# Down product with features on rows, row maxima on VectorE, in a LoRA feed-forward kernel

## The chip, the cores and the metric

One Trainium2 chip (trn2), one core. The metric is device time in microseconds (us). A core has TensorE (PE: matmuls from SBUF into PSUM), VectorE (DVE), ScalarE (ACT), GpSimd (POOL) and SyncE (SP, which here only starts transfers), each with its own instruction queue, working in order and meeting through semaphores.

## What is computed

`x` has 128 entries of 32 tokens with 512 features. Each entry has a LoRA index. Cut to what matters:

```python
gate = x @ W_gate.T + lora(x, A_gate, B_gate)     # 512 -> 1376, rank 16, by entry
up   = x @ W_up.T   + lora(x, A_up,   B_up)
act  = silu(gate) * up
down = act @ W_down.T + lora(act, A_down, B_down) # 1376 -> 512
amax = clip(max(abs(down), axis=-1), 1e-5)        # one value per token
out  = (down / amax) @ levels[weight_2bit].T * (amax * weight_scale) + bias
return x + out
```

The indices are sorted at run time, and the branch that this input takes treats tiles of 512 tokens with at most two LoRAs each ("wide" in the code).

## The kernel before

**Tiles and chunks.** 4,096 tokens make 8 wide tiles (0 to 7). The 1,376 hidden features make 11 chunks (0 to 10; chunk 0 has 96 features and 32 rows for the down product's LoRA). Every float32 operand is split into a hi and a lo part, and a product is three matmuls (hi x hi, lo x hi, hi x lo). All weights stay in SBUF from tile 0 on. Tiles 1 to 7 are one loop on TensorE, ScalarE and VectorE (lines 1924, 1106, 1485); SP and GpSimd have a loop for tiles 1 to 6 and written-out code behind it.

**TensorE in a chunk f** (`wide_tile`, L1871): 12 matmuls for gate (`pw_gate`), one for its LoRA, then a wait for the product of the chunk before (`act_done`, since `pw_up` is one bank), 12 for up, one LoRA, then for chunk f - 1 the A-down LoRA (`pw_td`, L1822) and 12 matmuls of the down product (`wide_down`, L1832). There a block s of 128 tokens of the activations is the stationary operand and the weights `wd` move, so that `pw_down[:, s, :]` holds tokens on partitions. Chunk 0's down product comes last, early in the next tile (`wide_first_down`, L1843).

**Behind the down product**, spread over the next tile, in chunks counted by f: ScalarE drains the four blocks from PSUM (f = 0, L1036). VectorE takes each token's largest absolute value, clamps it, inverts it and scales it (`wide_scales`, L1399, f = 0 to 3). ScalarE normalises (L1040, f = 1 to 4). In chunks 2, 4, 6, 8 TensorE transposes a block by four matmuls against the identity into `ps_misc` (L1856), ScalarE and VectorE split the transposed block into `wdt_split` (L1045, L1415), and in chunks 3, 5, 7, 9 TensorE multiplies it by the 2-bit weights `wq` (`wide_ffn`, L1863, "FFN block"). VectorE scales the result and adds the residual (`wide_output`, L1420), and SP stores it.

**VectorE in a chunk**, in this order: product gate x up (`wide_product`, L1387), lo half of the LoRA B matrix of chunk f + 2 (L1341), lo half of the activation (L1394), split of A-down (`wide_ad_split`, L1347: a cast and a subtraction), and then what the list above puts there.

**SP's queue in a tile** (L691 to L712): x for the next tile (16 loads, each with a look-up of its place in the plan), `wa_raw`, the mask, B-down, the other LoRA rows; between them the four outputs' stores, the residual of blocks 2 and 3 right behind stores 0 and 1; at the end a wait for all stores, a mask (L687 to L689), and the residuals of blocks 0 and 1 of this tile (L711). **GpSimd in a tile** (L826): once `wa_raw` is there, the A split (`wide_split_a`, 4 + 4 short operations, L794 and L799), the B-down split (L808, L811), then the bias added to each of four residual blocks (L817).

**Memory.** `rows` is [128, 6, 512]: blocks 0 to 3 are `wnorm` and `wout`, 4 and 5 the residuals `wx_res`.

Of the kernel before, what the change touches and what calls it, by code (L numbers as in the profile page):

```python
# [7 lines left out]
F32 = mybir.dt.float32  # L8
# [6 lines left out]
P = 128  # L15
# [54 lines left out]
PLAN_COLUMNS_STEP = 8  # L70
WQ_FROM = FC - KC
# [11 lines left out]
def build(nc, x_tok, x_feat, lora_index, places, pair_masks, w_gu, w_down, w_2bit, a_gu, a_down, b_rows,  # L83
          scale_col, bias_rows,
          block_mask_in, identity_in, out):
    with ExitStack() as ctx:
# [73 lines left out]
        with ExitStack() as wide:  # L160
# [8 lines left out]
            wact_split = sb("wact_split", [P, 2, 2, WIDE], F32R, stack=wide)  # L169
            wdt_split = sb("wdt_split", [P, 2, KC, P], F32R, stack=wide)  # L170
# [9 lines left out]
            wact_full = sb("wact_full", [P, 2, WIDE], stack=wide)  # L180
            pw_down = ps("pw_down", [P, WSUBS, 512], stack=wide)
# [11 lines left out]
        t_full = wact_full[0:PAIR, :, :]  # L193
        wnorm = rows[:, 0:WSUBS, :]
        wout = rows[:, 0:WSUBS, :]
        wx_res = rows[:, WSUBS:WSUBS + 2, :]
        x_late = [half.rearrange("p e n -> p (e n)").rearrange("p (s h) -> p s h", s=2)
# [58 lines left out]
        amax_steps = sem("amax_steps")  # L256
        drained = sem("drained")
# [129 lines left out]
        def store_wide(eng, tile, s, entries=range(SUB_ENTRIES)):  # L387
            store_wide_at(eng, tile, s, entries, block_places(eng, tile, s, entries))
# [4 lines left out]
        def store_wide_at(eng, tile, s, entries, places):  # L393
            eng.wait_ge(out_ready, WSUBS * tile + s + 1)
            for e, place in zip(entries, places):
                eng.dma_start(out[bass.ds(place, 1), :, :].rearrange("a t n -> (a t) n"),
                              wout[e * SEQ:(e + 1) * SEQ, s, :]).then_inc(stored, 16)
# [69 lines left out]
        def _(sp):  # L467
# [148 lines left out]
            def wide_residual(tile, s, dst, done, behind=False):  # L616
                entries = [entry_at(sp, wide_place(tile, SUB_ENTRIES * s + e)) for e in range(SUB_ENTRIES)]
                if behind:

                    sp.wait_ge(out_ready, WSUBS * tile + s - 1)  # L620
# [4 lines left out]
            def wide_program():  # L625
# [51 lines left out]
                for s in range(2):  # L677
                    wide_residual(0, s, wx_res[:, s, :], wxres_in[s])

                def outputs_of(tile, s):  # L680
# [10 lines left out]
                with sp.Fori(1, WTILES - 1) as tile:  # L691
# [19 lines left out]
                    for s in range(2):  # L711
                        wide_residual(tile, s, wx_res[:, s, :], wxres_in[s])  # L712
# [6 lines left out]
                for s in range(WSUBS):  # L719
                    outputs_of(last - 1, s)  # L720
                end_of(last)
                places = [block_places(sp, last, s, entries) for s, entries in enumerate(LAST_BY_SP)]
                for s, entries in enumerate(LAST_BY_SP):
                    store_wide_at(sp, last, s, entries, places[s])
# [128 lines left out]
        def _(act):  # L853
# [182 lines left out]
            def wide_drain(tile, s):  # L1036
                act.wait_ge(blocks_done, WSUBS * tile + s + 1)
                nc.scalar.activation(wnorm[:, s, :], pw_down[:, s, :], ACT.Copy).then_inc(drained, 1)

            def wide_normalise(tile, s, source):  # L1040
                act.wait_ge(rinv_ready, WSUBS * tile + s + 1)
                nc.scalar.activation(wnorm[:, s, :], source[:, s, :], ACT.Copy, scale=rinv[:, s:s + 1]
                                     ).then_inc(norm_ready, 1)

            def wide_dt_hi(tile, s, bank, dt):  # L1045
                act.wait_ge(transposed, WSUBS * tile + s + 1)
# [3 lines left out]
            def wide_tile(tile, first):  # L1050
# [28 lines left out]
                for f in range(FC):  # L1079
# [9 lines left out]
                    if not first and f == 0:  # L1089
                        for s in range(WSUBS):  # L1090
                            wide_drain(tile - 1, s)
# [4 lines left out]
                    if not first and 1 <= f <= WSUBS:  # L1096
                        wide_normalise(tile - 1, f - 1, wnorm)
                    if not first and f in (2, 4, 6, 8):

                        if f > 2:  # L1100
                            act.wait_ge(ffn_done, WSUBS * (tile - 1) + f // 2 - 1)
                        wide_dt_hi(tile - 1, f // 2 - 1, ps_misc[:, :], wdt_split)

            def wide_program():
# [14 lines left out]
                wide_normalise(last, 0, pw_down)  # L1119
                wide_normalise(last, 1, pw_down)  # L1120
                wide_dt_hi(last, 0, last_bank[0], last_dt(0))
                wide_normalise(last, 2, pw_down)
                wide_dt_hi(last, 1, last_bank[1], last_dt(1))
                wide_normalise(last, 3, pw_down)
                wide_dt_hi(last, 2, last_bank[2], last_dt(2))
                wide_dt_hi(last, 3, last_bank[3], last_dt(3))
                for s, entries in enumerate(LAST_BY_ACT):
                    if len(entries) > 0:
                        store_wide_at(act, last, s, entries, places[s])
# [19 lines left out]
        def _(dve):  # L1149
# [249 lines left out]
            def wide_scales(tile, s, source):  # L1399
                done = 2 * (WSUBS * tile + s)  # L1400
                if source is pw_down:
                    dve.wait_ge(blocks_done, WSUBS * tile + s + 1)
                else:
                    dve.wait_ge(drained, WSUBS * tile + s + 1)
                nc.vector.tensor_reduce(amax[:, s:s + 1], source[:, s, :], AX_X, ALU.max,
                                        apply_absolute_value=True).then_inc(amax_steps, 1)
                dve.wait_ge(amax_steps, done + 1)
                nc.vector.tensor_scalar(amax[:, s:s + 1], amax[:, s:s + 1], EPS, None, ALU.max
                                        ).then_inc(amax_steps, 1)
                dve.wait_ge(amax_steps, done + 2)  # L1410
# [4 lines left out]
            def wide_dt_lo(tile, s, bank, dt):  # L1415
# [598 lines left out]
```

## Time and profile before

| | us |
|---|---|
| Median of 3 runs | 911.34 (910.3 to 911.4) |
| The profiled execution, its own time | 911.69 |
| Its span in the profile | 909.8 |
| TensorE busy | 891.7 |
| VectorE, ScalarE, GpSimd busy | 349.3, 260.3, 82.4 |
| Mean granted TensorE clock, share of full speed | 0.996 |

Start times count from the start of the span. A row of a timeline gives start, duration, engine, line, operation, output <- inputs, shape, how many instructions are merged in it, and in brackets the idle time before it with what ended it. PE is a matmul, and its durations overlap by the pipeline's depth, so the pace is read from starts. `rows` is also the name of the SBUF buffer. "xN" is a count.

### The profile page before, as it was taken

The numbers are of one execution on the slowest core, as the hardware profiler recorded it, in microseconds if no ns is written. First come the engines' busy times: TensorE is split into PE (matmuls) and PEld (weight loads), VectorE is DVE, ScalarE is ACT, GpSimd is POOL, SyncE is SP. The second block draws the span as 40 slices with busy tenths as digits, with TensorE's granted clock in tenths as the row PEclk, the third lists the DMA queues.
The fourth block names the chain that finished last, engine by engine and source line by source line (L and its number), as shares of the span: only waits on it lengthen the run. The fifth ranks groups of instructions, "written<-read, shape, count | busy, mean of one in ns | idle before, by whom it ended". The sixth has DMA issues, their size and how long they took to land.

```text
span 909.8 us, 13814 instructions
## 1 busy us (share of the span) xinstructions
PE 891.7 (98%) x3998; PEld 721.7 (79%) x3998; DVE 349.3 (38%) x757; ACT 260.3 (29%) x450; POOL 82.4 (9%) x114
## 2 busy tenths in 40 slices
PE   6899999999999999999999999999999999999997
PEld 6688888888888887888888888888888888888885
DVE  3664345222632334422353224533254322552225
ACT  2533252111522224211252113421134111422112
POOL 1011003000030000300003100031000210110200
PEclk9899999999999999999999999999999999999999
DMA  4564111111112011120111102111011111201001
GB/s 128 140 185 141 46 53 33 45 35 30 42 44 56 23 33 50 32 63 16 44 47 40 51 12 56 44 40 41 15 53 55 35 35 30 60 24 32 26 14 47
DMA packets 44997, 45.38 MB, mean 50 GB/s; under 512 B 13168, under 2 KB 31472, under 8 KB 44944
## 3 DMA queue, kind: packets, MB, share of 16 engines
q1 hardware_dynamic: 42640, 41.72, 16.8%
q10 hardware_dynamic: 2176, 2.89, 1.1%
q14 instruction: 43, 0.35, 0.1%
q0 software_dynamic: 128, 0.26, 0.1%
q8 instruction: 10, 0.16, 0.1%
HBM read 36.44 MB, written 8.39 MB: 49 GB/s over the span
## 4 chain that ended last, share of the span: by engine, by line
PE 95%; DVE 1%; SPq 1%; issue 1%; DMA 1%; ACT 1%; DVEq 0%
PE pw_up L1766 26%; PE pw_gate L1766 24%; PE pw_down L1839 24%; PE ps_misc L1867 6%; PE pw_td L1828 5%; PE pw_down L1852 2%; PE pw_up L1808 2%; PE ps_misc L1766 2%; PE pw_gate L1808 2%; PE ps_misc L1859 1%; DMA low_room<-pair_masks 1%; SPq L317 0%; SPq L329 0%; ACT wt_split L1003 0%; DMA plan_room<-places 0%
## 5 line engine op out<-in xcount | busy, mean ns | idle before, releaser
L1839 PE MATMUL pw_down<-wd,wact_split 128*128 128x512 f32 x960 | 232.5, 391 | 0.0
L1766 PE MATMUL pw_up<-wxs,wgu 128*128 128x512 f32 x948 | 229.4, 391 | 0.0
L1839 PEld LDWEIGHTS pw_down<-wd,wact_split 128*128 128x128 f32 x960 | 180.2, 188 | 44.5
L1766 PE MATMUL pw_gate<-wxs,wgu 128*128 128x512 f32 x864 | 213.6, 396 | 0.5 <-DVE wgu L1152 0.5
L1766 PEld LDWEIGHTS pw_up<-wxs,wgu 128*128 128x128 f32 x948 | 178.4, 188 | 38.6
L1766 PEld LDWEIGHTS pw_gate<-wxs,wgu 128*128 128x128 f32 x864 | 161.7, 190 | 34.5 <-DVE wgu L1152 1.2
L1391 DVE TENSOR_TENSOR wact_full<-pw_up,wact_full 128x512 f32<-128x512 f32 (+1 forms) x87 | 60.1, 690 | 295.8 <-PE pw_up L1808 293.6
L1022 ACT ACTIVATE wact_full<-pw_gate 128x512 f32<-128x512 f32 (+1 forms) x80 | 47.7, 596 | 277.3 <-PE pw_gate L1808 277.3
L1034 ACT ACTIVATE wact_split<-wact_full 128x512 fp32r<-128x512 f32 x80 | 50.5, 631 | 69.5 <-DVE wact_full L1391 69.4
L1396 DVE TENSOR_TENSOR wact_split<-wact_full,wact_split 128x512 fp32r<-128x512 f32 x80 | 55.6, 695 | 26.6 <-ACT wact_split L1034 26.4
L817 POOL TENSOR_TENSOR rows<-rows,bias 128x512 f32<-128x512 f32 x28 | 35.8, 1288 | 220.8 <-DMA rows<-x_tok 219.6
L1867 PE MATMUL ps_misc<-wq,wdt_split 128*128 128x512 f32 x224 | 55.3, 389 | 0.0
L1828 PE MATMUL pw_td<-wact_split,wad_split 128*32 128x512 f32 (+1 forms) x160 | 50.4, 396 | 0.0
L794 POOL TENSOR_TENSOR wgu_first<-wa_raw,scales 128x64 fp32r<-128x64 f32 x28 | 8.5, 335 | 448.9 <-DMA wa_raw<-a_gu 448.9
L1424 DVE SCALAR_TENSOR_TENSOR rows<-ps_misc,scales,rows 128x512 f32<-128x512 f32 x28 | 21.0, 751 | 73.3 <-PE ps_misc L1867 57.5
L1867 PEld LDWEIGHTS ps_misc<-wq,wdt_split 128*128 128x128 f32 x224 | 42.0, 188 | 8.7
L997 ACT ACTIVATE wb_split<-low_room 64x256 fp32r<-64x256 f32 x40 | 16.8, 420 | 97.2 <-PE pw_up L1808 97.2
L1808 PE MATMUL pw_up<-wt_split,wb_split 96*128 96x512 f32 (+1 forms) x87 | 34.3, 395 | 0.0
L1808 PE MATMUL pw_gate<-wt_split,wb_split 96*128 96x512 f32 (+1 forms) x80 | 31.8, 397 | 2.6 <-DVE wt_split L1371 2.6
L1417 DVE TENSOR_TENSOR wdt_split<-ps_misc,wdt_split 128x512 fp32r<-128x512 f32 x28 | 19.3, 690 | 37.5 <-ACT wdt_split L1047 37.5
L997 ACT ACTIVATE wb_split<-wb_raw 64x256 fp32r<-64x256 f32 (+1 forms) x48 | 18.6, 403 | 49.8 <-PE pw_up L1808 47.1
L1003 ACT ACTIVATE wt_split<-wact_full 32x512 fp32r<-32x512 f32 x32 | 20.2, 630 | 42.1 <-DVE wact_full L1366 41.6
(134 smaller groups left out, 673.0 us busy)
## 6 DMA issues: line engine op xcount, KB each, us to landing
out<-rows SPq DMA_DIRECT2D x121, 64.0 KB, 1.6
rows<-x_tok SPq DMA_DIRECT2D x112, 64.0 KB, 1.8
rows<-w_gu SPq DMA_DIRECT2D x8, 512.0 KB, 4.2
x_raw<-x_feat SPq DMA_DIRECT2D x60, 64.0 KB, 1.8
x_more<-x_feat SPq DMA_DIRECT2D x59, 64.0 KB, 1.7
wb_raw<-b_rows SPq DMA_DIRECT2D x32, 92.0 KB, 2.8
low_room<-b_rows SPq DMA_DIRECT2D x32, 80.0 KB, 2.5
rows<-w_down SPq DMA_DIRECT2D x9, 256.0 KB, 4.3
```

The lines of the kernel that those rows point to most:

```text
L817: pool.tensor_tensor(wx_res[:, s % 2, :], wx_res[:, s % 2, :], bias[:, :], ALU.add).then_inc(residual_biased, 1)
L997: nc.scalar.activation(wb_split[0:2 * PAIR, f % 2, :, 0:WIDTHS[f]], wb_raw_chunk(f), ACT.Copy).then_inc(b_hi, 1)
L1022: nc.scalar.activation(wact_full[0:w, f % 2, :], gate_bank(f)[0:w, :], ACT.Silu).then_inc(silu_done, 1)
L1034: nc.scalar.activation(wact(HI, f), wact_full[0:WIDTHS[f], f % 2, :], ACT.Copy).then_inc(act_hi, 1)
L1391: nc.vector.tensor_tensor(wact_full[0:w, f % 2, :], up_bank(f, first)[0:w, :], wact_full[0:w, f % 2, :], ALU.mult).then_inc(act_done, 1)
L1396: nc.vector.tensor_tensor(wact(LO, f), wact_full[0:WIDTHS[f], f % 2, :], wact(HI, f).bitcast(F32), ALU.subtract).then_inc(act_lo, 1)
L1424: nc.vector.scalar_tensor_tensor(wout[:, s, :], bank, ascale[:, s:s + 1], residual, ALU.mult, ALU.add).then_inc(out_ready, 1)
L1766: last = nc.tensor.matmul(bank, w, wxs[:, xp, k, :], start=(n == 0 and k == 0), stop=False, skip_group_check=(f == 0))
L1808: nc.tensor.matmul(bank[0:w, :], wb_split[0:STACK, f % 2, g, 0:w], wt_split[0:STACK, g, :], start=False, stop=True, skip_group_check=(f == ...
L1828: last = nc.tensor.matmul(pw_td[0:m, :], wad_split[0:w, f % 2, 0:m], wact(part, f), start=(f == 0 and part == HI), stop=(f == FC - 1 and p ...
L1839: last = nc.tensor.matmul(pw_down[:, s, :], wact(ap, f)[:, s * P:(s + 1) * P], wd[:, wp, f, :], start=(f == 1 and n == 0), stop=False)
L1867: last = nc.tensor.matmul(bank, dt[:, part, k, :], wq[:, k, :], start=(part == HI and k == 0), stop=(part == LO and k == KC - 1))
```

## The change

In tiles 0 to 6 the roles in the down product are swapped: `wd` is stationary and the activations move, so `pw_down[:, k, :]` holds 128 features on partitions and 512 tokens in its columns, which is how the FFN block needs them. The 28 blocks of transposes on TensorE are gone. The maxima over a token's 512 features now go across four chunks and 128 partitions: VectorE reduces over the four chunks (a read with a stride of 512 elements), transposes 32x32 blocks, reduces each run of 32, joins the four quadrants by copies to other partitions and maxima, inverts, spreads each value over 32 columns and transposes back, and multiplies the four chunks by the result (each step of this waits for the one before, by `max_steps`; the waits are left out below). ScalarE's and VectorE's splits into `wdt_split` read SBUF instead of PSUM. The output is written over its residual in `wx_res`, so a residual is loaded once the store of the block before it in that place has landed. Tile 7 keeps the old orientation and is written out behind TensorE's loop.

```diff
@@ scratch: shares its place with wdt_split
+            max_rooms = sb("max_rooms", [P, 2, WIDE], stack=maxima_first)
@@ SP
-                    if s < 2:
-                        wide_residual(tile, s + 2, wx_res[:, s, :], wxres_in[s], behind=True)
+                    if second_next:
+                        sp.wait_ge(stored, 16 * SUB_ENTRIES * (WSUBS * tile + s + 1))
+                        ahead, block = (tile, s + 2) if s < 2 else (tile + 1, s - 2)
+                        wide_residual(ahead, block, wx_res[:, s % 2, :], wxres_in[s % 2])
                 def end_of(tile):
-                    sp.wait_ge(stored, 16 * WENTRIES * tile)
                     sp.wait_ge(td_masked, tile)
                     load_mask(sp, tile, mask_d, mask_d_in)
@@ end of SP's loop
                     end_of(tile)
-                    for s in range(2):
-                        wide_residual(tile, s, wx_res[:, s, :], wxres_in[s])
@@ ScalarE
+            def wide_dt_hi(tile, s):
+                act.wait_ge(norm_ready, KC * (tile + 1))
+                if s > 0:
+                    act.wait_ge(ffn_done, WSUBS * tile + s)
+                nc.scalar.activation(wdt_split[:, HI, :, :], feat[:, :, s * P:(s + 1) * P], ACT.Copy
+                                     ).then_inc(dt_hi, 1)
-                    if not first and 1 <= f <= WSUBS:
-                        wide_normalise(tile - 1, f - 1, wnorm)
@@ VectorE
+            def max_of_chunks(tile):
+                dve.wait_ge(drained, KC * (tile + 1))
+                nc.vector.tensor_reduce(max_room, feat.rearrange("p k t -> p t k"), AX_X, ALU.max,
+                                        apply_absolute_value=True).then_inc(max_steps, 1)
+            def max_of_tokens(tile):
+                nc.vector.transpose(turned_room, max_room)
+                nc.vector.tensor_reduce(token_max, turned_room.rearrange("p (j c) -> p j c", c=SEQ), AX_X, ALU.max)
+                copy(other_max[0:64, :], token_max[64:128, :])
+                copy(other_max[64:128, :], token_max[0:64, :])
+                tt(token_max, token_max, other_max, ALU.max)
+                copy(other_max[0:32, :], token_max[32:64, :])
...
+                copy(other_max[96:128, :], token_max[64:96, :])
+                tt(token_max, token_max, other_max, ALU.max)
+                nc.vector.tensor_scalar(token_max, token_max, EPS, None, ALU.max)
+                nc.vector.reciprocal(token_inv, token_max)
+                for a in range(4):
...
+                    tt(ascale[quadrant, :], by_quadrant[quadrant, a, :],
+                       wscale[quadrant, :].to_broadcast([32, WSUBS]), ALU.mult).then_inc(ffn_scaled, 1)
+                copy(max_room.rearrange("p (j c) -> p j c", c=SEQ),
+                     token_inv[:, :, None].to_broadcast([P, WENTRIES, SEQ]))
+                nc.vector.transpose(turned_room, max_room)
+            def normalise(tile):
+                for k in range(KC):
+                    nc.vector.tensor_tensor(feat[:, k, :], feat[:, k, :], turned_room, ALU.mult
+                                            ).then_inc(norm_ready, 1)
@@ VectorE, order in a chunk
                     if f < FC - 2:
                         wide_b_lo(tile, f + 2)
+                    if not first and f == 0:
+                        max_of_chunks(tile - 1)
                     if f < FC - 1:
                         wide_act_lo(tile, f)
                         wide_ad_split(tile, f + 1, first)
-                    if not first and f < WSUBS:
-                        wide_scales(tile - 1, f, wnorm)
+                    if not first and f == 1:
+                        max_of_tokens(tile - 1)
+                    if not first and f == 2:
+                        normalise(tile - 1)
@@ TensorE
+                for k in range(KC):
+                    for n, (ap, wp) in enumerate(PASSES):
+                        last = nc.tensor.matmul(pw_down[:, k, :], wd[:, wp, f, k * P:(k + 1) * P], wact(ap, f),
+                                                start=(f == 1 and n == 0), stop=False)
-                    if not first and f in (2, 4, 6, 8):
...
-                        wide_transposes(tile - 1, f // 2 - 1, ps_misc[:, :])
-                with pe.Fori(1, WTILES) as tile:
+                with pe.Fori(1, last) as tile:
                     wide_tile(tile, False)
-                last = WTILES - 1
+                wide_tile(last, False, by_token=True)
```

## Rows read from the trace of the kernel before

**Rows 1.** The page, parts 1 and 4: busy times, chain by engine.

```profile
PE 891.7 (98%) x3998; PEld 721.7 (79%) x3998; DVE 349.3 (38%) x757; ACT 260.3 (29%) x450; POOL 82.4 (9%) x114
...
PE 95%; DVE 1%; SPq 1%; issue 1%; DMA 1%; ACT 1%; DVEq 0%
```

**Rows 2.** Groups by line and form, TensorE; behind the bar busy us, mean ns.

```profile
L1859 PE MATMUL ps_misc<-identity,rows 128*128 128x128 f32 x116 | 17.4, 272 | 0.0
```

**Rows 3.** Timeline of TensorE, tile 3, chunks 2 to 4.

```profile
360.29 2.90 PE L1766 MATMUL pw_up<-wxs,wgu 128*128 128x512 f32 x12
...
366.91 0.60 PE L1859 MATMUL ps_misc<-identity,rows 128*128 128x128 f32 x4
...
370.33 2.90 PE L1766 MATMUL pw_up<-wxs,wgu 128*128 128x512 f32 x12
...
376.53 1.98 PE L1867 MATMUL ps_misc<-wq,wdt_split 128*128 128x512 f32 x8
378.34 2.88 PE L1766 MATMUL pw_gate<-wxs,wgu 128*128 128x512 f32 x12
...
381.29 2.90 PE L1766 MATMUL pw_up<-wxs,wgu 128*128 128x512 f32 x12
```

**Rows 4.** Timeline of ScalarE, tile 3, chunk 0: the four drains.

```profile
352.25 2.65 ACT L1038 ACTIVATE rows<-pw_down 128x512 f32<-128x512 f32 x4
```

**Rows 5.** Timeline of VectorE, tile 3, around the product of chunk 2.

```profile
364.31 0.68 DVE L1405 TENSOR_REDUCE scales<-rows 128x1 f32<-128x512 f32 x1
365.03 0.15 DVE L1408 TENSOR_SCALAR scales<-scales 128x1 f32<-128x1 f32 x1
...
365.35 0.69 DVE L1391 TENSOR_TENSOR wact_full<-pw_up,wact_full 128x512 f32<-128x512 f32 x1
366.07 0.42 DVE L1343 TENSOR_TENSOR wb_split<-wb_raw,wb_split 32x256 fp32r<-32x256 f32 x1
366.81 0.69 DVE L1396 TENSOR_TENSOR wact_split<-wact_full,wact_split 128x512 fp32r<-128x512 f32 x1 [0.33 <-ACT wact_split L1034]
367.42 0.17 DVE L1357 CAST wad_split<-wad_raw 128x32 fp32r<-128x32 f32 x1
...
367.74 0.68 DVE L1405 TENSOR_REDUCE scales<-rows 128x1 f32<-128x512 f32 x1
```

**Rows 6.** Timeline of GpSimd, tile 7, B-down's lo half and two bias additions.

```profile
794.72 1.77 POOL L811 TENSOR_TENSOR wd<-low_room,wd 32x512 fp32r<-32x512 f32 x1
796.57 2.59 POOL L817 TENSOR_TENSOR rows<-rows,bias 128x512 f32<-128x512 f32 x2
```

**Rows 7.** Groups by line and form, VectorE: a one-source pass.

```profile
L1165 DVE TENSOR_SCALAR wq<-rows 128x512 fp32r<-128x512 int32 x4 | 1.7, 419 | 0.0
```

**Rows 8.** Timeline of VectorE, tile 7, the same moments as rows 6.

```profile
794.64 0.69 DVE L1396 TENSOR_TENSOR wact_first<-wact_full,wact_first 96x512 fp32r<-96x512 f32 x1 [2.51 <-ACT wact_first L1034]
795.25 1.27 DVE L1357 CAST wad_split<-wad_raw 128x32 fp32r<-128x32 f32 x1
```

**Rows 9.** Timeline of SP's queue, from the end of tile 2 into tile 3.

```profile
337.88 0.35 SPq L384 DMA_DIRECT2D low_room<-pair_masks  x1
341.01 6.42 SPq L622 DMA_DIRECT2D rows<-x_tok  x8
...
371.39 0.85 SPq L333 DMA_DIRECT2D wa_raw<-a_gu  x2
```

**Rows 10.** Timeline of GpSimd, tile 3.

```profile
373.69 1.23 POOL L794 TENSOR_TENSOR wgu_first<-wa_raw,scales 128x64 fp32r<-128x64 f32 x4 [71.45 <-DMA wa_raw<-a_gu]
...
376.71 1.04 POOL L808 TENSOR_TENSOR wd<-low_room,scales 32x512 fp32r<-32x512 f32 x1 [0.22 <-POOL wgu_first L799]
377.82 1.29 POOL L811 TENSOR_TENSOR wd<-low_room,wd 32x512 fp32r<-32x512 f32 x1
```

**Rows 11.** Timeline of GpSimd, tile 1: the first operation of its A split.

```profile
145.65 1.05 POOL L794 TENSOR_TENSOR wgu_first<-wa_raw,scales 128x64 fp32r<-128x64 f32 x4 [71.47 <-DMA wa_raw<-a_gu]
```

**Rows 12.** Timeline of TensorE, tile 1: the first block of transposes.

```profile
147.32 0.60 PE L1859 MATMUL ps_misc<-identity,rows 128*128 128x128 f32 x4
```

More of the change, by code:

```diff
@@ L70 @@
 PLAN_COLUMNS_STEP = 8
+MAX_STEPS = 11
 WQ_FROM = FC - KC
@@ L1089, in wide_tile @@
                     if not first and f == 0:
-                        for s in range(WSUBS):
-                            wide_drain(tile - 1, s)
+                        for k in range(KC):
+                            wide_drain(tile - 1, k)
                     if f < FC - 1:
@@ L1835, in wide_down, with wide_first_down, down_by_token @@
                 elif f == 1:
-                    pe.wait_ge(drained, WSUBS * tile)
+                    pe.wait_ge(drained, KC * tile)
+                for k in range(KC):
+                    for n, (ap, wp) in enumerate(PASSES):
+                        last = nc.tensor.matmul(pw_down[:, k, :], wd[:, wp, f, k * P:(k + 1) * P], wact(ap, f),
+                                                start=(f == 1 and n == 0), stop=False)
+                last.then_inc(down_done, 1)
+            def wide_first_down(tile):
+                pe.wait_ge(bd_ready, tile + 1)
+                pe.wait_ge(td_ready, tile + 1)
+                for k in range(KC):
+                    for n, (ap, wp) in enumerate(PASSES):
+                        last = nc.tensor.matmul(pw_down[:, k, :], wd[:, wp, 0, k * P:(k + 1) * P],
+                                                wact_first[:, ap, :], start=False, stop=(n == 2))
+                    last.then_inc(blocks_done, 1)
+            def down_by_token(f):
+                if f == 1:
+                    pe.wait_ge(drained, KC * (WTILES - 1))
                 for s in range(WSUBS):
@@ L1869, in wide_ffn, with wide_tile @@
                 last.then_inc(ffn_done, 1)
-            def wide_tile(tile, first):
+            def wide_tile(tile, first, by_token=False):
                 if first:
@@ L1907, in wide_tile @@
                     wide_lora_a_down(tile, f - 1)
-                    wide_down(tile, f - 1, first)
-                    if not first and f in (2, 4, 6, 8):
-                        if f == 2:
+                    if by_token:
+                        down_by_token(f - 1)
+                    else:
+                        wide_down(tile, f - 1, first)
+                    if not first and f in (3, 5, 7, 9):
+                        if f == 3:
                             pe.wait_ge(silu_done, FC * tile + 2)
@@ L1914, in wide_tile @@
                             pe.wait_ge(out_ready, WSUBS * (tile - 1) + f // 2 - 1)
-                        wide_transposes(tile - 1, f // 2 - 1, ps_misc[:, :])
-                    if not first and f in (3, 5, 7, 9):
                         wide_ffn(tile - 1, f // 2 - 1, ps_misc[:, :], wdt_split)
```

175 lines of the change are left out of this document (104 added, 71 removed).

## The prediction

> **What bounds the kernel now.** I read the page first. TensorE is busy for 98% of the span and carries 95% of the chain that ended last [rows 1]. So a microsecond of work taken off TensorE is a microsecond off the time, and work on any other engine is free until TensorE has to wait for it. The group list then shows what the change takes away: short matmuls against the identity. 116 of them write `ps_misc` [rows 2]; four of these belong to the last tile, which keeps its transposes, so 112 go, in 28 blocks of four. Next I read TensorE's timeline of one tile in the steady state (tile 3), to see what four of them really occupy and by when TensorE will want each input [rows 3]. Last come the timelines of VectorE, GpSimd and the DMA queue, because the change puts a long chain on VectorE and moves GpSimd's work against it [rows 4 to 12]. All clock times below are those of tile 3, "in its frame".
>
> **What TensorE saves.** In the same place of a chunk, 3.42 us pass from the start of the transposes to the start of the following up product (366.91 to 370.33). Behind an FFN block, with no transposes, the same gate product and its LoRA matmul take 2.95 us (378.34 to 381.29) [rows 3]. So a block costs 0.47 us: about 0.35 for the four themselves and 0.12 for the slower start behind them. 28 blocks x 0.47 = **13.2 us saved**. The down product keeps its count and shape (12 matmuls of 128x512 per chunk, only the operands' roles swapped); I take its pace as unchanged. ScalarE loses four normalisations per tile; it was never late, so that is worth nothing. The last tile written out after the loop and the tail itself are costed at nothing: matmuls, counts and waits there stay, and tile 0 is already written out that way.
>
> **What VectorE gets in chunk 0: one reduction of 2,048 elements.** It starts when the four drains end at 354.90 (352.25 + 2.65) [rows 4]. Its price is in no row. The contiguous 512-element reduction takes 0.68 us [rows 5], about 0.14 fixed and 0.53 streaming, so from below 4 x 0.53 + 0.14 = 2.3 us. From above I take GpSimd's pace, the slowest of the trace for 512 columns: two bias additions take 2.59 us [rows 6], 2.5 ns an element, or 5.1 us. Nearest is the same engine's own reduction, so 2.3. Behind it stand the lo half of the activation and the A-down split, 0.93 us (as 366.81 to 367.74 [rows 5]), then the product of chunk 1, 0.69, and about 0.15 for TensorE to see it: 354.95 + 2.3 + 0.9 + 0.7 + 0.15 = 359.0. TensorE wants it at 360.29 [rows 3]. The cover is 1.3 us, so the reduction is free up to 3.6 us.
>
> Here every element of the source lies 2 KB behind the one before, and no row shows such a read. The Trainium skill (Vector Engine (DVE) Microarchitecture Reference, section 5.2, Measured stream behaviour on trn2) gives 1.73 ns a column where a source hops every element, which by its figure makes an estimate of 3.6 us: just at the edge of the cover, and the sum below would grow by about 1 us over seven tiles. No run here shows it yet.
>
> **What VectorE gets in chunk 1: the chain of 20 small steps.** It stands ahead of chunk 2's product. Today the scales for one block start at 364.31 and that product starts at 365.35 [rows 5]. A step that depends on the one before costs its duration plus 0.03 to 0.04 (364.31 to 365.03 for one of 0.68). So does one that starts at other partitions than its predecessor (365.35 to 366.07 for one of 0.69), while others follow after 0.61 (366.81 to 367.42) [rows 5]. Hence: block transpose, priced as a 512-element pass, and the segmented reduction, 2 x 0.72; nine steps on 16 columns (two quadrant copies, maximum, four copies, maximum, clamp) at 0.15 + 0.04 each, 1.7; reciprocal and four scale products, 0.85; broadcast copy, 0.42 as the one-source pass at that size [rows 7] + 0.03; second transpose, 0.61. Sum 5.0 us against 1.04 today. If the small ones overlapped it would be 4.3; with a transpose at twice the price, 6.1. Chunk 2's product then starts at 369.4, ends at 370.1 and reaches TensorE at 370.2. Without the transposes TensorE wants it at 370.33 - 0.47 = 369.86. **Wait: about 0.35 us in each of seven tiles.**
>
> **What VectorE gets in chunk 2: four multiplications, and who is in their way.** 2.39 us after the product's start (365.35 to 367.74 [rows 5]), at 371.8 to 372.1, the four multiplications of 128x512 with two SBUF inputs begin. Alone they need 2.5 us, then ScalarE's hi half 0.75, VectorE's lo half (now also from two SBUF inputs) 0.7, and TensorE could start the FFN block at about 376.2. It wants to at 370.2 + 6.20 = 376.4 (today 370.33 to 376.53 [rows 3]). Covered, with 0.2 to 0.5 to spare, while nothing disturbs them.
>
> GpSimd does. The trace shows that the two engines take turns: a cast of 0.17 us took 1.27 and ended when GpSimd's subtraction ended (795.25 + 1.27 = 796.52; 794.72 + 1.77 = 796.49), and that subtraction had itself waited for VectorE's activation split that ended at 795.33 [rows 6, 8]; 1.29 is its time in tile 3 [rows 10]. Held are VectorE's operations with two SBUF inputs and its casts; I take the reductions and those with a PSUM input as free, since they stand at their usual times beside GpSimd's.
>
> Where does GpSimd's work fall? It waits for `wa_raw`, which SP's queue reaches last. SP's queue today goes from the mask at 337.88 over four place look-ups (to 341.01, 2.8 us) and eight residual loads with four more look-ups (6.42 us) to the 16 x loads and `wa_raw` at 371.39 [rows 9]. The change spreads the residual loads behind the stores; at the end of a tile four remain, ahead of the mask. Half of 2.8 + 6.4 goes: everything behind is 4.6 us earlier. GpSimd then starts at 373.69 - 4.6 = 369.1: small splits until 371.9, B-down hi half at 376.71 - 4.6 = 372.1 (1.04), lo half (1.29) and two bias additions (2.6 together) [rows 6, 10]. That is exactly on the four multiplications. Taking turns from 372.1: multiplication to 372.8, hi half to 373.7, multiplication to 374.3, lo half to 375.4, multiplication to 376.0, bias to 377.2, multiplication to 377.7, ScalarE to 378.5, second bias until 378.9, VectorE's lo half to 379.4, TensorE at 379.6. **Wait: 379.6 - 376.4 = 3.2 us** in each of tiles 3 to 6.
>
> The other tiles differ. Tile 1: GpSimd starts 1.7 us ahead of the transposes' place (145.65 against 147.32 [rows 11, 12]) and is not moved, so its small splits and then its four long operations meet the chain of small steps instead. The splits add some 0.1 us to each of nine steps, and each long one lets one step by: 0.35 + 0.5 + 1.04 + 1.29 + 2.6 minus what is left of the splits' cover makes about 5.4. Tile 2: the loop's first round is about 1 us later, two long operations meet the multiplications: 1.3 + 0.4 = 1.7. Tile 7: no A split; the B-down split and bias stand until 799.2 [rows 6] against the end of chunk 0, where the lo half and the cast each wait for one: 1.0 + 0.35 = 1.4.
>
> **Sum.** -13.2 + 4 x 3.55 + 5.4 + 1.7 + 1.4 = **+9.5 us**. The profiled execution took 911.69 (span 909.8), so it would take 921.2; the median of the runs shown is 911.34, 0.35 lower, and gives 920.8. I say 921.
>
> **Rivals.**
> 1. The work moved off TensorE stays hidden: GpSimd and VectorE miss each other, because the DMA queue is not earlier or because turns are not one for one. For it: VectorE is busy for 38% of the span [rows 1] and the holds are few today. Against: the eight loads are in the queue's rows, and so is the hold [rows 6, 8, 9]. Then 911.3 - 13.2 + 7 x 0.35 = 900.6, or 898.1 if the chain takes under 4.7 us. Chance 0.27. This is the one on the other side; it decides at GpSimd's start: later than about 371.5 in tile 3's frame and the multiplications are through.
> 2. The chain is shorter (4.3 us, small steps overlapping). The multiplications then start 0.8 us earlier and two get by: wait 1.6 in tiles 3 to 6, 2.7 in tile 1, 0.4 in tile 2, 0.9 in tile 7, together 10.4: 908.5. Chance 0.13, with sizes from 904 to 914.
> 3. The strided reduction becomes a bound: at GpSimd's pace of 5.1 us TensorE waits 1.5 us more per tile, 10.7 in all, on top of the forecast 931, without the clash 911. Or a block transpose at twice the price, +1.1 per tile, 928. By the Trainium skill's 1.73 ns, above, it just stays covered. Chance 0.12.
> 4. The change doesn't do what it says: TensorE's down product runs at another pace with weights and activations swapped, or the written-out last tile stalls on its code. All shapes and the instruction count per chunk stay; chance 0.03, a few us either way.
> The forecast itself has 0.45.
>
> **Numbers.** The likeliest case gives 921; its own range is 914 to 928, from GpSimd's start 1 us later (wait 1.8 instead of 3.6) to a longer chain. For 8 in 10 it must reach to rival 1 at 900 and up to 929. A measurement of this kernel tells about 0.2% (1.8 us) from no change. Faster: rival 1, most of rival 2 and a part of 3, 0.37. Same: 0.05. Slower: 0.58.
>
> **What would show it.** In the new trace: per block 0.47 us less between a down product and the next up product; TensorE idle ahead of the up product of chunk 2 by about 0.35 us behind VectorE's product; idle ahead of the FFN block of chunk 3 by 2 to 4 us behind VectorE's lo half, with multiplications of 1.2 to 1.8 us instead of 0.7, each ending in step with a GpSimd operation; GpSimd's A split starting 4 to 5 us earlier in tiles 2 to 6; a 5 us wait in tile 1 at the up product of chunk 2. I am wrong if the multiplications stand at 0.7 us each, if the chain is under 4.3 us, or if the reduction of chunk 0 takes over 3.6 us.

## The result, and the profile after

| | median of its runs, us | ratio to the kernel before, 95% interval |
|---|---|---|
| before | 911.37 (910.3 to 911.92) | |
| after | 937.41 (933.32 to 938.15) | 1.0278 [1.0247, 1.0309] |

The change costs 2.8%. The prediction said 921 in a range of 900 to 929, so the sign was right and the size was not. The profiled run of after took 937.84 us, with a span of 936.1.

The page of after, parts 1, 2 (the clock line) and 4. They answer to [rows 1]:

```profile
PE 895.6 (96%) x3886; PEld 718.7 (77%) x3886; DVE 416.3 (44%) x806; ACT 239.7 (26%) x422; POOL 83.9 (9%) x114
...
PEclk9899998999999999999998999999999899999999
...
PE 84%; DVE 9%; issue 3%; ACT 1%; SPq 1%; DMA 1%; DVEq 0%; ACTq 0%
```

112 matmuls are gone, and yet TensorE is busy 4 us longer than before (895.6 against 891.7). Fewer instructions with more busy time means that some of them ran slower. VectorE now has 9% of the chain, where it had 1%.

TensorE's timeline of after, tile 3, chunks 2 to 4. It answers to [rows 3]; tile 3 lies 9.54 us later than before (first down product at 360.83 against 351.29).

```profile
366.86 2.90 PE L1840 MATMUL pw_gate<-wxs,wgu 128*128 128x512 f32 x12
...
369.87 3.01 PE L1840 MATMUL pw_up<-wxs,wgu 128*128 128x512 f32 x12
...
376.60 2.88 PE L1840 MATMUL pw_gate<-wxs,wgu 128*128 128x512 f32 x12
379.32 0.39 PE L1882 MATMUL pw_gate<-wt_split,wb_split 96*128 96x512 f32 x1
379.89 3.06 PE L1840 MATMUL pw_up<-wxs,wgu 128*128 128x512 f32 x12 [0.18 <-DVE wact_full L1410]
...
383.48 2.92 PE L1914 MATMUL pw_down<-wact_split,wd 128*128 128x512 f32 x12
389.59 3.44 PE L1959 MATMUL ps_misc<-wq,wdt_split 128*128 128x512 f32 x8 [3.19 <-DVE wdt_split L1470]
392.87 2.91 PE L1840 MATMUL pw_gate<-wxs,wgu 128*128 128x512 f32 x12
```

Two waits are to be seen: a small one ahead of chunk 2's up product, and 3.19 us ahead of the FFN block. Then comes what the prediction did not have: the same eight matmuls of the FFN block take 3.44 us where they took 1.98 [rows 3].

VectorE's and GpSimd's timelines of the same stretch of after (they answer to [rows 5, 10]):

```profile
364.48 3.82 DVE L1421 TENSOR_REDUCE max_rooms<-rows 128x512 f32<-128x2048 f32 x1 [1.98 <-ACT rows L1054]
...
374.00 0.70 DVE L1430 STREAM_TRANSPOSE max_rooms<-max_rooms 128x512 f32<-128x512 f32 x1
374.74 0.69 DVE L1432 TENSOR_REDUCE maxima<-max_rooms 128x16 f32<-128x512 f32 x1
375.46 0.17 DVE L1435 COPY maxima<-maxima 64x16 f32<-64x16 f32 x1
...
377.22 0.25 DVE L1449 RECIPROCAL maxima<-maxima 128x16 f32<-128x16 f32 x1
377.39 0.67 DVE L1454 TENSOR_TENSOR scales<-maxima,scales 32x4 f32<-32x4 f32 x4
...
379.18 0.65 DVE L1410 TENSOR_TENSOR wact_full<-pw_up,wact_full 128x512 f32<-128x512 f32 x1
...
381.22 1.02 DVE L1376 CAST wad_split<-wad_raw 128x32 fp32r<-128x32 f32 x1
...
382.39 5.76 DVE L1465 TENSOR_TENSOR rows<-rows,max_rooms 128x512 f32<-128x512 f32 x4
388.85 0.69 DVE L1470 TENSOR_TENSOR wdt_split<-rows,wdt_split 128x512 fp32r<-128x512 f32 x1 [0.69 <-ACT wdt_split L1061]
```
```profile
378.38 1.05 POOL L807 TENSOR_TENSOR wgu_first<-wa_raw,scales 128x64 fp32r<-128x64 f32 x4 [62.74 <-DMA wa_raw<-a_gu]
379.39 1.36 POOL L812 TENSOR_TENSOR wgu_first<-wa_raw,wgu_first 128x64 fp32r<-128x64 f32 x4
380.97 1.24 POOL L821 TENSOR_TENSOR wd<-low_room,scales 32x512 fp32r<-32x512 f32 x1 [0.22 <-POOL wgu_first L812]
382.28 1.34 POOL L824 TENSOR_TENSOR wd<-low_room,wd 32x512 fp32r<-32x512 f32 x1
383.81 3.19 POOL L830 TENSOR_TENSOR rows<-rows,bias 128x512 f32<-128x512 f32 x2 [0.19 <-POOL wd L824]
```

The four multiplications take 5.76 us, and they lie beside GpSimd's long operations. GpSimd starts 17.55 us after the tile's first down product (360.83 to 378.38); before it was 22.40 (351.29 to 373.69).

Last, TensorE's granted clock (the column behind POOL's busy time) in windows of after, around the FFN block of tile 3 and that of tile 4:

```profile
386.30:389.60 3.30, 0.11 (x2) 0.01 (x1) 2.60 (x4) 1.42 (x3) 0.70 (x1) 0.92 0.00 0
389.60:393.00 3.40, 3.40 (x9) 2.73 (x10) 1.93 (x5) 0.63 (x1) 0.00 (x0) 0.57 0.00 0
503.06:507.00 3.94, 3.94 (x9) 3.14 (x10) 1.96 (x6) 0.64 (x2) 0.00 (x0) 0.50 0.00 0
507.00:510.00 3.00, 3.00 (x11) 2.39 (x10) 0.73 (x1) 0.00 (x0) 0.00 (x0) 0.74 0.00 0
510.00:514.00 4.00, 4.00 (x19) 3.13 (x19) 0.26 (x1) 0.87 (x2) 0.00 (x0) 1.00 0.00 0
```

TensorE does nothing from 386.40 to 389.59. The mean of 0.92 in its window says that the clock fell before the FFN block began. Over the block the mean is 0.57 of full speed, in tile 4 it is 0.50 (1.2 GHz of 2.4) for the whole block and well into the gate product behind it. Then it is back at 1.00.

**Where the 26.3 us of span went.** The start of one tile's first down product to the next one's gives each tile's length. A tile of before takes 109.79; with nothing in TensorE's way the changed one takes 107.88 (experiment 3 below). What each tile of after has above that:

| tile of after | 1 | 2 | 3 | 4 | 5 | 6 | 7 |
|---|---|---|---|---|---|---|---|
| length, us | 114.82 | 113.67 | 113.35 | 114.65 | 113.57 | 114.86 | |
| above 107.88 | 6.94 | 5.79 | 5.47 | 6.77 | 5.69 | 6.98 | 1.4 |

Together 39.0. The 1.4 of tile 7 is what is left for it and for all behind it: 1.2 up to its own chunk 0 down product (at 917.68), 0.2 behind that. With tile 0 (0.6 longer, within what its end moves in the traces shown here, 130.35 to 132.34) and 7 x 1.91 = 13.4 saved, that is +26.3, the whole difference. How the 39.0 divide into waits and clock is read from starts: a down product to its FFN block, 6.11 (383.48 to 389.59) where 2.76 is the undisturbed pace, so 3.35 of wait; the block itself 3.28 (389.59 to 392.87) where 1.81 is [rows 3], so 1.47 of clock.

### The profile page after: what moved, and what is told of

The parts are those of the page before. It is cut to its first block, busy times and chain, and to the rows that moved or that the text cites. A ratio compares the mean times of both kernels' runs of the same rounds, so it can differ in the third digit from the quotient of the medians.

```text
span 936.1 us, 13633 instructions
## 1 busy us (share of the span) xinstructions
PE 895.6 (96%) x3886; PEld 718.7 (77%) x3886; DVE 416.3 (44%) x806; ACT 239.7 (26%) x422; POOL 83.9 (9%) x114
## 4 chain that ended last, share of the span: by engine, by line
PE 84%; DVE 9%; issue 3%; ACT 1%; SPq 1%; DMA 1%; DVEq 0%; ACTq 0%
PE pw_up L1840 24%; PE pw_gate L1840 21%; PE pw_down L1914 17%; PE ps_misc L1959 7%; PE pw_td L1902 4%; DVE rows L1465 3%; PE pw_down L1934 2%; PE pw_down L1924 2%; PE ps_misc L1840 2%; PE pw_up L1882 2%; PE pw_gate L1882 2%; DVE wad_split L1376 1%; DVE scales L1454 1%; DVE wact_full L1410 1%; DVE max_rooms L1430 1%
## 5 line engine op out<-in xcount | busy, mean ns | idle before, releaser
L1840 PE MATMUL pw_up<-wxs,wgu 128*128 128x512 f32 x948 | 233.6, 396 | 5.8 <-DVE wact_full L1410 5.8
L1914 PE MATMUL pw_down<-wact_split,wd 128*128 128x512 f32 x840 | 203.3, 391 | 0.0
L1840 PEld LDWEIGHTS pw_gate<-wxs,wgu 128*128 128x128 f32 x864 | 166.2, 192 | 37.0 <-DVE wgu L1171 1.5
L1914 PEld LDWEIGHTS pw_down<-wact_split,wd 128*128 128x128 f32 x840 | 157.7, 188 | 38.9
L1959 PE MATMUL ps_misc<-wq,wdt_split 128*128 128x512 f32 x224 | 63.5, 431 | 16.2 <-DVE wdt_split L1470 16.2
L1959 PEld LDWEIGHTS ps_misc<-wq,wdt_split 128*128 128x128 f32 x224 | 46.5, 210 | 28.4 <-DVE wdt_split L1470 18.3
L830 POOL TENSOR_TENSOR rows<-rows,bias 128x512 f32<-128x512 f32 x28 | 39.0, 1404 | 296.2 <-DMA rows<-x_tok 294.9
L1465 DVE TENSOR_TENSOR rows<-rows,max_rooms 128x512 f32<-128x512 f32 x28 | 33.8, 1266 | 0.0
L1421 DVE TENSOR_REDUCE max_rooms<-rows 128x512 f32<-128x2048 f32 x7 | 26.9, 3837 | 13.9 <-ACT rows L1054 13.9
```

The lines of the kernel that those rows point to most:

```text
L830: pool.tensor_tensor(wx_res[:, s % 2, :], wx_res[:, s % 2, :], bias[:, :], ALU.add).then_inc(residual_biased, 1)
L1421: nc.vector.tensor_reduce(max_room, feat.rearrange("p k t -> p t k"), AX_X, ALU.max, apply_absolute_value=True).then_inc(max_steps, 1)
L1465: nc.vector.tensor_tensor(feat[:, k, :], feat[:, k, :], turned_room, ALU.mult).then_inc(norm_ready, 1)
L1840: last = nc.tensor.matmul(bank, w, wxs[:, xp, k, :], start=(n == 0 and k == 0), stop=False, skip_group_check=(f == 0))
L1914: last = nc.tensor.matmul(pw_down[:, k, :], wd[:, wp, f, k * P:(k + 1) * P], wact(ap, f), start=(f == 1 and n == 0), stop=False)
L1959: last = nc.tensor.matmul(bank, dt[:, part, k, :], wq[:, k, :], start=(part == HI and k == 0), stop=(part == LO and k == KC - 1))
```

## The experiments

The ratios stand against 911.73 us (experiments 1 to 4) and 911.57 us (5 and 6) of the kernel before, run on the same chip beside them. The changed kernel was not run beside them; what is said against "after" is against the 937.41 and the trace shown above.

**1. GpSimd's work held back** in each tile of its loop, until VectorE has made the lo half of that tile's first block.

```diff
                 with pool.Fori(1, WTILES - 1) as tile:
+                    pool.wait_ge(dt_lo, WSUBS * tile - 3)
```

> The changed kernel; GpSimd only starts its work of a tile in the loop once VectorE has made the lo half of the first block. Nothing is left out. Theory A (VectorE and GpSimd take turns, and GpSimd's long operations fell on the four multiplications): multiplications 0.7 us each instead of 1.27, no wait ahead of the FFN block of chunk 3, no low clock; waits left are 0.15 ahead of the up product of chunk 2 and about 0.5 ahead of that of chunk 3, so 911.4 - 13.2 + 7 x 0.6 = about 902 us. Rival B (VectorE's chain is too long by itself, whoever runs beside it): the multiplications speed up little, the wait of 3.3 us stays in tiles 2 to 6, and the time is 930 us or more.

Measured: **903.29 us** (902.03 to 904.25), ratio 0.9912 [0.9895, 0.9929]: 34 us less than after, and faster than before. VectorE's and TensorE's timelines in tile 3:

```profile
369.31 2.49 DVE L1466 TENSOR_TENSOR rows<-rows,max_rooms 128x512 f32<-128x512 f32 x4
```
```profile
367.66 3.02 PE L1841 MATMUL pw_up<-wxs,wgu 128*128 128x512 f32 x12 [0.18 <-DVE wact_full L1411]
...
371.21 2.92 PE L1915 MATMUL pw_down<-wact_split,wd 128*128 128x512 f32 x12
373.97 1.98 PE L1960 MATMUL ps_misc<-wq,wdt_split 128*128 128x512 f32 x8
```

With GpSimd silent there the four multiplications take 2.49 us instead of 5.76. The FFN block neither waits nor runs slow. What is left is the small wait of chunk 2 and a slightly slower up product in chunk 1, and the tiles are 108.5 long. So the clash of the two engines carries both the waits and what follows them.

**2. TensorE kept busy through the wait**: twelve matmuls whose result nobody reads, ahead of the FFN block of chunk 3. The edit leaves the waits on VectorE as they are.

```diff
                         if f == 3:
                             pe.wait_ge(silu_done, FC * tile + 2)
+                            if not by_token:
+                                for _ in range(12):
+                                    nc.tensor.matmul(ps_misc[:, :], wd[:, HI, 1, 0:P], wd[:, HI, 1, :],
+                                                     start=True, stop=True)
```

> The changed kernel; TensorE runs 12 matmuls of 128x512 (2.7 us) into ps_misc, which nobody reads, in the place where it waits for the FFN block of chunk 3, in tiles 1 to 6. They fit into the wait of 3.3 us in tiles 2 to 6 and cost 2.7 us in tile 1, which has no such wait. Theory C (what the waits do not explain is TensorE's clock, which falls to half behind an idle stretch of 3 us): the FFN block takes 2.0 us instead of 3.4 to 3.8, the gate product behind it 2.9 instead of up to 4.0, the granted clock stays at 1.00 there; 5 tiles x about 2.1 us less and 2.7 more, so about 930 us. Rival D (the slow FFN block is late operands or memory): FFN block stays at 3.4 to 3.8 us and the time is 937.4 + 2.7 = 940 us.

Measured: **927.54 us** (924.47 to 929.3), ratio 1.0176 [1.0152, 1.02], 9.9 us less than after. More work on the engine that bounds the kernel made it faster. TensorE's timeline in tile 3, then a window over the FFN block:

```profile
382.36 2.92 PE L1914 MATMUL pw_down<-wact_split,wd 128*128 128x512 f32 x12
385.12 2.88 PE L2010 MATMUL ps_misc<-wd 128*128 128x512 f32 x12
387.87 2.14 PE L1959 MATMUL ps_misc<-wq,wdt_split 128*128 128x512 f32 x8
389.85 2.90 PE L1840 MATMUL pw_gate<-wxs,wgu 128*128 128x512 f32 x12
```
```profile
385.00:388.00 3.00, 3.00 (x15) 2.28 (x14) 2.30 (x3) 1.42 (x3) 2.27 (x2) 1.00 0.10 22
388.00:392.00 4.00, 4.00 (x18) 3.27 (x19) 2.50 (x6) 0.63 (x1) 0.00 (x0) 1.00 0.00 0
```

The FFN block of tile 3 starts 5.51 us behind its down product (382.36 to 387.87) against 6.11. But the clock stays at 1.00, and the block takes 2.14 us instead of 3.44. In tiles 4 and 5 the block is just as late as in after (6.19 and 6.17 against 6.22 and 6.14), and runs at full pace all the same. Tile 4:

```profile
499.98 2.11 PE L1959 MATMUL ps_misc<-wq,wdt_split 128*128 128x512 f32 x8 [0.55 <-DVE wdt_split L1470]
```

Tiles 2 to 6 became 11.6 us shorter together. By starts, 1.7 of that are blocks that began earlier (0.4 to 0.7 each in tiles 2, 3 and 6, nothing in 4 and 5), and 9.8 the clock. Tile 1, which has no wait at this place, became 2.2 longer: the added work is 2.7, its own wait is 0.2 longer and the slow stretch behind that 0.7 shorter.

**3. No chain on VectorE**: maxima, reciprocal and the four multiplications left out (one count that the last tile's transposes wait for is fitted to it, not shown).

```diff
             def wide_dt_hi(tile, s):
-                act.wait_ge(norm_ready, KC * (tile + 1))
+                act.wait_ge(drained, KC * (tile + 1))
...
-                    if not first and f == 0:
-                        max_of_chunks(tile - 1)
...
                     if not first and f == 1:
-                        max_of_tokens(tile - 1)
-                    if not first and f == 2:
-                        normalise(tile - 1)
+                        for a in range(4):
+                            q = slice(32 * a, 32 * (a + 1))
+                            nc.vector.tensor_copy(ascale[q, :], wscale[q, :].to_broadcast([32, WSUBS])
+                                                  ).then_inc(ffn_scaled, 1)
```

> The changed kernel without VectorE's maxima, reciprocals and multiplications in tiles 1 to 7 of the loop: rows are not normalised and the output scale is the weight scale alone. Shows what TensorE's side is worth when nothing waits: theory (28 blocks of transposes at 0.47 us, swapped roles of the operands cost nothing) 911.4 - 13.2 = 898.2 us. Rival (the swapped down product or the written-out last tile is slower on TensorE): over 900 us, with down products of over 2.73 us start to start.

Measured: **897.53 us** (897.08 to 899.31), ratio 0.9856 [0.9837, 0.9876]. Every tile takes 107.88 (first down products at 346.11 and 453.99, for one): 1.91 less than before, 0.478 per block. That is the saving on TensorE by itself, and it shows that the down product with its operands swapped keeps its pace (in after too: 373.87 to 376.60, 2.73 us, as 364.18 to 366.91 in before).

**4. Can the chain be kept and the waits not?** Experiment 1, with two moves more: the four scale products go behind the four multiplications, and the strided reduction goes to chunk 1, behind that chunk's product.

```diff
-                by_quadrant = token_max.rearrange("p (s a) -> p a s", a=4)
-                for a in range(4):
-                    quadrant = slice(32 * a, 32 * (a + 1))
-                    tt(ascale[quadrant, :], by_quadrant[quadrant, a, :],
-                       wscale[quadrant, :].to_broadcast([32, WSUBS]), ALU.mult).then_inc(ffn_scaled, 1)
...
                     nc.vector.tensor_tensor(feat[:, k, :], feat[:, k, :], turned_room, ALU.mult
                                             ).then_inc(norm_ready, 1)
+                by_quadrant = token_max.rearrange("p (s a) -> p a s", a=4)
+                for a in range(4):
+                    quadrant = slice(32 * a, 32 * (a + 1))
+                    nc.vector.tensor_tensor(ascale[quadrant, :], by_quadrant[quadrant, a, :],
+                       wscale[quadrant, :].to_broadcast([32, WSUBS]), ALU.mult).then_inc(ffn_scaled, 1)
...
-                    if not first and f == 0:
+                    if not first and f == 1:
                         max_of_chunks(tile - 1)
```

> As e1_pool_late, and VectorE's order changed in two places: the four scale products behind the multiplications instead of in the chain, and the strided reduction behind the product of chunk 1 instead of ahead of it. Nothing is left out. Theory: the reduction (3.8 us) and the chain (now about 4.5 us) both lie inside TensorE's cover, no wait is left in tiles 1 to 6, so about 898.5 us, faster than before by 1.4%. Rival: the reduction now delays the activation's lo half of chunk 1 and TensorE waits ahead of the A-down matmuls of chunk 2, 0.5 us a tile or more, so 902 us or more.

Measured: **897.8 us** (896.65 to 898.79), ratio 0.985 [0.9831, 0.9869]. Tiles take 107.88 again. This version beats both kernels, before by 13.9 us and after by 39.6. Which of the two moves took away how much was not tried apart; in the trace of experiment 1 the reduction's share is 0.13 a tile and the chain's 0.46. GpSimd's late start costs nothing: an output of VectorE now waits for its bias additions, and TensorE does not wait for the output. VectorE's timeline of experiment 4, tile 3:

```profile
367.42 2.49 DVE L1461 TENSOR_TENSOR rows<-rows,max_rooms 128x512 f32<-128x512 f32 x4
369.83 0.70 DVE L1466 TENSOR_TENSOR scales<-maxima,scales 32x4 f32<-32x4 f32 x4
...
378.39 0.75 DVE L1495 SCALAR_TENSOR_TENSOR rows<-ps_misc,scales,rows 128x512 f32<-128x512 f32 x1 [4.50 <-POOL rows L830]
```

**5. Only SP's queue later.** Experiment 1 shows that the clash costs the time, not why GpSimd is early. Here GpSimd has no new wait; SP gets seven look-ups more at the end of a tile.

```diff
+                    for e in range(7):
+                        entry_at(sp, wide_place(tile, e))
```

> The changed kernel (937.4 us) with seven place look-ups more in SyncE's loop, whose results nobody uses, behind the last store of a tile. In the kernel before each look-up took SyncE about 0.7 us, and in the changed kernel GpSimd's elementwise work starts 4.85 us earlier in a tile because SyncE issues its load that much earlier. Theory (the clash of VectorE's four multiplications with GpSimd comes from that earlier start alone): GpSimd starts some 4.9 us later again, the multiplications stand at about 0.7 us each instead of 1.27, the wait of 3.2 us ahead of the FFN block of tiles 2 to 6 goes or falls to 0.3 us, and with it the block's slow clock; five tiles times (3.2 + 1.5 to 2.5) is 23 to 28 us less, so 909 to 914 us, about 911. Tile 1 keeps its wait of 4.3 us. Rival (GpSimd's start hangs on something else, or the multiplications are slow by themselves): the time stays at 937 within 1 us.

Measured: **908.74 us** (907.78 to 910.49), ratio 0.9973 [0.9964, 0.9983]. In tile 3 GpSimd starts 21.39 us behind the first down product (354.31), 3.84 later than in after. GpSimd's and VectorE's rows there, then TensorE's, one of tile 1 and one of tile 3:

```profile
375.70 2.47 POOL L809 TENSOR_TENSOR wgu_first<-wa_raw,scales 128x64 fp32r<-128x64 f32 x4 [66.61 <-DMA wa_raw<-a_gu]
```
```profile
375.08 2.69 DVE L1467 TENSOR_TENSOR rows<-rows,max_rooms 128x512 f32<-128x512 f32 x4
```
```profile
154.22 5.23 PE L1842 MATMUL pw_up<-wxs,wgu 128*128 128x512 f32 x12 [4.33 <-DVE wact_full L1412]
...
379.78 1.98 PE L1961 MATMUL ps_misc<-wq,wdt_split 128*128 128x512 f32 x8
```

The multiplications have begun 0.6 us before GpSimd, meet its short splits instead of its long operations, and lose 0.2 us together. Tiles 2 to 6 fall to 108.50 to 108.57. Tile 1 keeps its 114.79, with the wait and the slow product. So a few microseconds of queue time on SP, an engine that computes nothing, decide over 28.7 us.

**6. Only tile 1.** GpSimd waits once, ahead of its loop, for the lo half of the first block (one, not three, as the expectation below says).

```diff
+                pool.wait_ge(dt_lo, 1)
                 with pool.Fori(1, WTILES - 1) as tile:
```

> The changed kernel (937.4 us) with one wait more: GpSimd's loop over tiles does not begin until VectorE has finished the first three bf16 remainders of tile 1, so that GpSimd starts late in tile 1 alone. Theory (in tile 1 the up product waits 4.25 us, and runs 5.27 instead of 2.9 us behind that, because VectorE's activation steps take turns with GpSimd): both go, 4.3 + 2.4 = 6.7 us less, about 930.7 us, and the waits of 3.2 us in tiles 2 to 6 stay. Rival (the wait of tile 1 is the chain of small steps itself, or the delay only moves the clash to a later step of tile 1 or into tile 2): 935 to 938 us.

Measured: **929.03 us** (928.05 to 932.28), ratio 1.0206 [1.0186, 1.0226]. Tile 1 goes from 114.82 to 108.56, that is 6.3 us (6.7 were expected). The waits of tiles 2 to 6 stay, as TensorE's waits of this run show (total, times, longest):

```profile
PE ps_misc L1960 <- DVE wdt_split L1471: 15.6, 5, 3.3
```

The profiled spans differ by 9.6 us (936.1 and 926.5): 6.3 in tile 1, 1.3 in tile 0, and 2.1 in tiles 2 to 6, where single tiles are up to 1.7 shorter and one is 1.3 longer. The slow stretch behind a wait of the same size is not of the same length each time, and in tile 2 of this run it is missing. TensorE's FFN block there, and the window over it and the start of the gate product:

```profile
268.42 2.11 PE L1960 MATMUL ps_misc<-wq,wdt_split 128*128 128x512 f32 x8 [3.27 <-DVE wdt_split L1471]
```
```profile
268.42:271.42 3.00, 3.00 (x13) 2.50 (x14) 2.60 (x6) 0.64 (x2) 0.00 (x0) 1.00 0.00 0
```

The block is 3.43 us late by starts, as in after, TensorE stood idle for 3.27, and the clock is at 1.00: the block takes 2.11. So lateness does not slow the block, and an idle stretch of this length does not always bring the clock down. In the traces of after and of experiments 2, 5 and 6 TensorE waits 13 times for 2.5 to 4.4 us in tiles 1 to 6, and the clock falls in 12 of them, one of 2.53 us among them (tile 4 here). What decides is not shown.

## Why the prediction was right and wrong

**The saving: right.** 13.2 forecast, 7 x 1.91 = 13.4 measured.

**The strided reduction: mis-sized.** Forecast 2.3 us, measured 3.82, over the 3.6 up to which the prediction called it free, which was one of its signs of being wrong. It makes chunk 1's up product about 0.15 late in each tile (369.87 less 366.86 is 3.01, and the product takes 3.01 instead of 2.90), 1.0 us in all. The Trainium skill (Vector Engine (DVE) Microarchitecture Reference, section 5.2) was the better guide: by its figure for a source that hops 4 KiB (here it is 2 KB), 2,048 elements at 1.73 ns plus the 0.14 fixed make an estimate of 3.7 (the prediction wrote 3.6), and the trace comes near it with 3.82.

**The chain: right.** Forecast 5.0, measured 5.18 (374.00 to 379.18). The block transpose that no row had shown costs 0.70, as assumed, and the small steps that depend on each other did not overlap (0.17 plus 0.03 to 0.04). The chain has 18 steps, not the 20 of the heading; the sum had counted them rightly. The wait of 0.35 was there (0.34 by starts, 3.29 against 2.95). Reduction and chain together cost 0.62 per tile (108.50 against 107.88, experiments 1 and 3). That fell to nothing in experiment 4.

**The clash with GpSimd in tiles 3 to 6: right in mechanism and size.** GpSimd's start was forecast at 369.1 and came at 368.8 in that frame (378.38 - 9.54); multiplications from 372.1, came at 372.85; 5.6 us for the four, came 5.76; a wait of 3.2, came 3.35. Who met whom was one place off: GpSimd's first long operation held the cast (1.02 instead of 0.17), the next three held a multiplication each, the fourth multiplication and the lo half ran free. The prediction had the cause too: residual loads leave SP's queue ahead of the x loads, so that `wa_raw` comes earlier. SP's row of after for tile 3 is

```profile
376.08 0.85 SPq L350 DMA_DIRECT2D wa_raw<-a_gu  x2
```

which is 366.54 in that frame, 4.85 earlier than the 371.39 of [rows 9] (forecast 4.6). With the look-ups' time given back (experiment 5) the clash is gone. The Trainium skill (GPSIMD Engine Reference, section 1) says that VectorE's operations with two SBUF inputs contend with GpSimd for SBUF; here three of tile 3's four multiplications took 1.76 to 1.78 us each, and the undisturbed fourth 0.68, so the trace agrees.

**Tile 2: mis-sized.** "The loop's first round is about 1 us later" gave 1.7 for it. In before that was so (GpSimd 23.58 us behind the first down product, not 22.40), but in after the delay is gone: it starts at 17.67, as in tile 3, and tile 2 waits like the others, 4.1 in all. **Tile 1: right in kind**, 4.7 instead of 5.4. VectorE's timeline in tile 1 of after shows the chain caught beside GpSimd:

```profile
150.05 3.64 DVE L1454 TENSOR_TENSOR scales<-maxima,scales 32x4 f32<-32x4 f32 x4
```

Four products of four columns, 0.67 in tile 3, take 3.64: three of them end with a long operation of GpSimd, and the second, between two such, takes 0.15. GpSimd's first long one held the maximum ahead of them (0.90 instead of 0.17). Tile 7 was forecast at 1.4, and is at 1.4. All waits together, with the slower start behind them: 22.7 forecast, 26.2 measured, so these terms are short by 3.5: 2.4 in tile 2 and 1.8 in tiles 3 to 6, less 0.7 in tile 1.

**The step that failed is the sum itself.** "4 x 3.55 + 5.4 + 1.7 + 1.4" counts a microsecond of waiting as a microsecond, and puts the clock behind the waits at nothing, without a reason. In all six tiles with a wait of over 3 us TensorE came back at half its clock. Summed from starts, as above for tile 3, the slow stretches behind the waits cost 2.25 (tile 1), 1.7, 1.5, 2.7, 1.7 and 2.9 = 12.8 us. Waits short by 3.5, a clock of 12.8 not counted and 0.6 in tile 0, less 0.2 of saving, are 16.7: from 921.2 to the profiled 937.8. Without the clock it would be 925.1, inside the range. Experiment 2 shows that it is the idle time and not the lateness: there the blocks of tiles 4 and 5 are as late as in after, TensorE is busy but for the last 0.6 us, and of the 10.5 us of clock in tiles 2 to 6 9.8 are gone.

The rows to see it by were in the trace of before. Its timeline of TensorE in tile 0:

```profile
32.50 0.54 PE L1808 MATMUL pw_gate<-wt_split,wb_split 96*96 96x512 f32 x1 [2.58 <-DVE wt_split L1371]
...
34.78 5.25 PE L1766 MATMUL pw_gate<-wxs,wgu 128*128 128x512 f32 x12 [0.46 <-DVE wgu L1152]
```

Twelve matmuls that take 2.90 elsewhere take 5.25 here, shortly behind 2.58 us of idle time (the granted clock is 0.54 in the mean over these 5.25 us). I read [rows 3] from a tile in the steady state, where TensorE never stands still, and so had no such row. The Trainium skill (TensorE: Matmul & The Clock Gate, Part 1, What's actually happening) gives the same two levels and says that an idle TensorE falls to the lower; these rows and the six waits of after agree, tile 2 of experiment 6, idle for 3.27 us at a clock of 1.00, does not.

**Rivals.** Rival 1, no clash, did not happen; experiment 5 makes it happen in five tiles and gives 908.7, and experiment 1 in six, 903.3, against its 900.6. Its deciding point was put at 371.5 in tile 3's frame; in experiment 5 GpSimd starts at 372.7 there (375.70 less 3.02) and the multiplications are through. Whether 371.5 would do was not tried. Rival 2, a chain of 4.3, fell with the 5.18. Rival 3 had the reduction at 5.1: it took 3.82.

## What to carry to other kernels

When a forecast puts a wait of some microseconds on TensorE, look in the trace for a row behind an idle stretch of that length and add what it shows, as a range: in after each of the long waits cost its 3.4 to 4.4 us and another 1.5 to 2.9 for the clock, and in experiment 6 one such wait cost nothing for the clock. Waits of 0.2 to 0.5 us had no such tail. When VectorE gets work with two SBUF inputs, find out where GpSimd's work lies and what starts it, even a queue that computes nothing; if GpSimd's results are wanted late, one wait that puts it behind the critical chain may be worth more than the change itself (937.4 to 903.3, and 897.8 with two steps more put where nobody waits for them).

## What the runs showed of the hardware that I had not expected

- The clock: behind 3.2 us of idle time TensorE mostly came back at its lower level (a mean of 0.50 to 0.57 in the windows above), and the slow stretch had not the same length in each tile (1.5 to 2.9 us lost behind waits of 3.19 to 3.30, nothing behind one of 3.27 in experiment 6, 1.7 behind one of 2.53 there).
- A matmul group that starts right behind a short wait takes 3.01 to 3.06 us instead of 2.90. A wait of 0.18 in the profile's brackets is 0.34 by starts, and the slower group behind it adds some 0.1.
- Turns are taken by small operations too: a product of 32x4 elements waits for the end of GpSimd's running operation (3.64 us for four, above). Which operations meet decides: in experiment 5, beside GpSimd's short splits, VectorE lost 0.2 us on the multiplications (2.69 against 2.49), and the four splits took 2.47 instead of 1.05.
